# Attention on one Trainium2 core: scores in two pairs of PSUM banks, everything else in one shared bank, xn and y turned by DMA as fp16 halves

## The reference

```
x = x + attention(layernorm(x))     # 16 heads of 16 channels, causal, rotation by head index
x = x + moe(layernorm(x))           # shared SwiGLU + 8 experts, top 2 per token
attention: q, k, v = split(xn @ W_attn + b); softmax(q k^T / 4, causal) v; y @ W_proj + b_proj
```

## Time and profile before

| | |
|---|---|
| median of 3 runs | 1647.81 us (1647.56 to 1649.53) |
| profiled execution | 1641.4 us, its span 1639.7 us |
| mean granted TensorE clock | 0.976 |
| busy over the span | PE 1506.1 us (92%), DVE 1045.2 (64%), ACT 828.9 (51%), POOL 895.8 (55%) |
| attention stage | to about 814 us of the span; then shared and routed experts |

### The profile page before, as it was taken

How to read it: one execution, slowest core, us unless ns; L and a number is a source line. 1 busy time by engine, 2 the same in 40 slices (tenths; PEclk the granted TensorE clock), 3 DMA queues, 4 the chain that set the end, 5 groups by cost and what they waited for, 6 DMA issues and landing times.

```text
span 1639.7 us, 41525 instructions
## 1 busy us (share of the span) xinstructions
PE 1506.1 (92%) x14714; PEld 1099.9 (67%) x14716; DVE 1045.2 (64%) x1828; ACT 828.9 (51%) x1252; POOL 895.8 (55%) x1121
## 2 busy tenths in 40 slices
PE   3689999999999999987699999999999999999995
PEld 2345555555555555543577888889888888888884
DVE  7567888888888888877468887743333333333332
ACT  1266666666666666655223335534444444444442
POOL 2144555555555555544131777747666666666663
PEclk9699999999999999999699999999999999999998
DMA  2333333333333333344867954446666666666662
GB/s 84 97 92 91 116 99 115 106 104 117 94 109 112 110 105 111 97 118 103 169 164 213 221 114 99 92 111 104 105 99 101 101 99 105 98 103 97 103 101 37
DMA packets 283156, 181.03 MB, mean 110 GB/s; under 512 B 160625, under 2 KB 273649, under 8 KB 282962
## 3 DMA queue, kind: packets, MB, share of 16 engines
q1 hardware_dynamic: 244370, 130.25, 31.4%
q0 software_dynamic: 30016, 35.55, 14.9%
q10 hardware_dynamic: 8576, 12.58, 2.4%
HBM read 83.91 MB, written 60.17 MB: 88 GB/s over the span
## 4 chain that ended last, share of the span: by engine, by line
PE 62%; DVE 9%; DMA 9%; SPq 6%; issue 5%; POOL 4%; ACT 4%; ACTq 0%; POOLq 0%; DVEq 0%
PE bank L1582 19%; PE pair_s L1856 12%; PE bank L1717 6%; PE bank L1856 6%; PE pair_t L1856 6%; SPq L442 4%; PE pair_s L1644 4%; DMA qk_d<-qkl 3%; PE bank L1752 3%; PE pair_t L1691 3%; ACT prob L883 2%; DMA k_op<-qk_d 2%; POOL prob L685 1%; DVE early L1503 1%; POOL tok_d L767 1%
## 5 line engine op out<-in xcount | busy, mean ns | idle before, releaser
L883 ACT ACTIVATE prob<-pair_t 128x1024 f32<-128x1024 f32 x320 | 327.8, 1024 | 228.6 <-PE pair_t L1691 223.8
L685 POOL TENSOR_SCALAR_AFFINE_SELECT prob<-prob 128x256 f32<-128x256 f32 (+1 forms) x448 | 198.5, 457 | 330.5 <-ACT prob L883 322.6
L808 POOL DMA_INDIRECT out_x<-ysb,tok_rows x135 | 217.1, 1608 | 156.5 <-ACT ysb L1019 107.6
L992 ACT CAST early<-early 128x512 f16<-128x512 f32 (+1 forms) x206 | 124.3, 603 | 324.1 <-DVE early L1503 302.0
L1509 DVE TENSOR_TENSOR early<-early 128x512 f16<-128x512 f32 (+1 forms) x206 | 138.9, 674 | 137.9 <-ACT early L992 135.2
L1503 DVE SCALAR_TENSOR_TENSOR early<-pair_s,h_s,sg 128x512 f32<-128x512 f32 (+1 forms) x103 | 75.2, 730 | 226.5 <-PE pair_s L1856 215.8
L1582 PE MATMUL bank<-wbuf,early 128*128 x1620 | 188.7, 273 | 4.7 <-DVE early L1509 3.4
L1856 PE MATMUL pair_s<-xt,wbuf 128*128 128x256 f16 x1704 | 188.7, 267 | 2.3 <-ACT sg L984 1.4
L767 POOL DMA_INDIRECT tok_d<-tok_w,dest_i x128 | 135.4, 1058 | 99.2 <-DVE dest_i L1426 58.2
L1717 PE MATMUL bank<-prob,v_op 128*32 128x512 f32 (+3 forms) x2048 | 178.8, 444 | 5.1 <-POOL prob L685 5.0
L1158 DVE TENSOR_REDUCE mx<-pair_s 128x2 f32<-128x1024 f32 x128 | 156.8, 1225 | 41.0 <-PE pair_s L1664 40.2
(11 more groups left out here) (272 smaller groups left out, 2735.9 us busy)
## 6 DMA issues: line engine op xcount, KB each, us to landing
q_op<-qk_d SPq DMA_DIRECT2D x192, 64.0 KB, 2.6
k_op<-qk_d SPq DMA_DIRECT2D x192, 64.0 KB, 2.7
x_in<-in_L_attn_x SPq DMA_DIRECT2D x16, 512.0 KB, 3.9
qk_d<-qkh SPq DMA_DIRECT2D x32, 256.0 KB, 2.2
qk_d<-qkl SPq DMA_DIRECT2D x32, 256.0 KB, 2.6
xres<-in_L_attn_x SPq DMA_DIRECT2D x16, 512.0 KB, 4.6
x_d<-x SPq DMA_DIRECT2D x32, 256.0 KB, 2.2
xhl_d<-xhl SPq DMA_DIRECT2D x32, 256.0 KB, 2.5
```

What stands on the lines that cost most here:

```text
L685: last = nc.gpsimd.affine_select(out=v, in_=v, compare_op=ALU.is_ge, fill=0.0, base=0, pattern=[[0, v.shape[1]], [1, P]], channel_multipli ...
L808: pool.indirect_dma_start(out=out, out_offset=bass.IndirectOffsetOnAxis(ap=tok_rows[:, block, 0:1], axis=0), in_=ysb[:, here], in_offset=N ...
L883: nc.scalar.activation(prob[:, half, u].rearrange("p a n -> p (a n)"), pair_t[:].rearrange("p a n -> p (a n)"), ACT.Exp, scale=exp_by).the ...
```

## The change

It is one rewrite of the attention stage's plan with these parts.

1. PSUM: banks 5 and 6 become `pair_u`, and scores alternate between `pair_s` and `pair_u`; they wait for the maximum of the unit two before. Everything else (q/k and v projections, maxima, o, output projection: 16 uses a batch) goes through bank 7, `ps_a`, each use waiting for the one that last emptied it.
2. xn is split into fp16 halves by POOL (`xn_split`, a cast and a subtraction for each of four tiles) and turned by one transposing DMA of 512 KB on SP (`xn_columns`); `transpose_xn`, `xn_high` and `xn_low` go. W_attn is split into scaled fp16 halves instead of fp32r.
3. y is split the same way (`y_split`) and turned by two transposing DMAs of 256 KB (`y_columns`); `transpose_y` and ACT's copy go. The output projection becomes 12 fp16 matmuls for each half in place of eight fp32 ones; W_proj is scaled and split once, and the scales are taken off in `values`, `divide` and `residual`.
4. Exponentials and selections run two whole groups back (10 units in place of 8), the value products of a group at (2 groups later, unit 3) and (3 groups later, units 0, 0 and 1).
5. All slots are set anew. Stores of q and k are at (2,0) and (2,4), their loads start in the same slots; xn is turned at (0,0), y at (3,1) and at (0,0) of the batch after.
6. Variances stay in one array `mv_all`, which saves a copy; PE waits for the last x1 ahead of the shared expert.

```diff
+        pair_of = (pair_s, pair_u)
+        ps_t, ps_o, ps_a = bank[2:4], bank[4], bank[7]
...
-        LAG, MAXIMA, M_ROWS, M_SP, O_OUT = 8, 0, 1, 2, 3
-        MIX = (0, 2, 2, 3)
-        XN_T, XN_HIGH, XN_LOW = ((0, 1), (0, 2)), ((0, 1), (0, 2)), ((0, 1), (0, 3))
-        QK, QK_ROWS = ((0, 4), (1, 4), (2, 4), (3, 1)), ((1, 0), (2, 0), (3, 0), (3, 4))
-        QK_HIGH, QK_LOW = ((1, 1), (2, 1), (3, 1), (0, 0)), ((1, 2), (2, 2), (3, 3), (0, 1))
-        V_PROJ, V_PROJ_B, VALUES = ((1, 2), (2, 1)), ((1, 3), (2, 1)), ((1, 3), (2, 3))
-        QK_STORE, QK_LOAD = ((2, 3), (0, 2)), ((2, 3), (0, 3))
-        STATS, VARIANCE, RSTD, SHIFT = ((1, 0), (1, 2)), (1, 4), (1, 4), (2, 1)
...
-        O_T = ((1, 4), (2, 2), (3, 2), (0, 1))
-        Y_T, Y_OUT = ((2, 3), (0, 3)), ((3, 1), (0, 4))
-        PROJ, PROJ_B = ((3, 3), (1, 1)), ((3, 4), (1, 1))
...
+        MAXIMA, M_ROWS, M_SP = 1, 1, 2
+        MIX, O_OUT = ((2, 3), (3, 0), (3, 0), (3, 1)), (3, 1)
+        XN_SPLIT, XN_COLUMNS = ((1, 2), (2, 0), (3, 2), (3, 4)), (0, 0)
+        QK = QK_ROWS = ((0, 4), (1, 2), (1, 4), (2, 0))
+        QK_HIGH, QK_LOW = ((1, 0), (1, 3), (2, 0), (2, 2)), ((1, 1), (1, 4), (2, 1), (2, 3))
+        V_PROJ = VALUES = ((2, 4), (3, 3))
+        QK_STORE = QK_LOAD = ((2, 0), (2, 4))
+        STATS, VARIANCE, RSTD, SHIFT = ((0, 3), (0, 4)), (0, 4), (0, 4), (1, 0)
+        NORMALISE = ((1, 0), (1, 3), (2, 3), (3, 0))
+        O_T = DIVIDE = ((2, 2), (2, 3), (3, 0), (3, 2))
+        Y_SPLIT, Y_COLUMNS = ((2, 4), (3, 0), (3, 1), (3, 3)), ((3, 1), (0, 0))
+        PROJ = ((3, 4), (0, 2))
+        X_BIAS = ((1, 0), (1, 3), (2, 2), (3, 1))
+        X1, X1_STATS, X1_VARIANCE = ((3, 4), (0, 2)), ((0, 0), (1, 1)), ((0, 0), (1, 2))
+        RSTD_B, ROWS = ((0, 0), (1, 2)), ((0, 1), (1, 4))
+        XRES, ROWS_OUT = (0, 3), ((1, 1), (3, 2))
...
+            def xn_columns(n):
+                sp.wait_ge(S["xnl_done"], NT * (n + 1))
...
+                    sp.wait_ge(S["qk_in"], 4 * n)
+                    sp.wait_ge(S["v_in"], 2 * n)
...
+                sp.dma_start_transpose(xn_t[:], xn_hl[:].rearrange("p t n -> p (t n)")).then_inc(S["xn_cols"], 16)
...
+            def y_columns(bp, j):
+                sp.wait_ge(S["yl_done"], 4 * bp + 2 * j + 2)
...
+                    sp.wait_ge(S["pr_in"], 2 * bp + j)
...
+                sp.dma_start_transpose(y_t[:], y_hl[:, j].rearrange("p t n -> p (t n)")).then_inc(y_turned[j], 16)
...
+                high = xn_hl[:, t, 0:C]
+                nc.gpsimd.tensor_copy(high, xn[:, t]).then_inc(S["xnh_done"], 1)
...
+                nc.gpsimd.tensor_tensor(xn_hl[:, t, C:], xn[:, t], high, ALU.subtract).then_inc(S["xnl_done"], 1)
...
-                if some(UN * G + u):
-                    pe.wait_ge(S["max_done"], UN * G + u)
+                if some(UN * G + u - 1):
+                    pe.wait_ge(S["max_done"], UN * G + u - 1)
+                pair_k = pair_of[(UN * G + u) % 2]
...
+            def project_out(bp, j, nxt):
+                pe.wait_ge(y_turned[j], 16 * bp + 16)
...
+                    last = products(ps_a[:, 256 * t:256 * t + 256],
+                                    [((y_t[:, 4 * t + c, :], y_t[:, 4 * t + CC + c, :]), (wp_h[:, c, :], wp_l[:, c, :]))
+                                     for c in range(CC)])
```

More of the change, by code:

```diff
@@ L467, in _ @@
                         load_qk(0, 0, j, third, a)
+            xn_columns(1)
             sp.dma_start(gate_t[:], gate_w).then_inc(S["misc_in"], 16)
@@ L509, in body @@
                             sp.dma_start(xres[:], xv[b - 1]).then_inc(S["res_in"], 16)
+                        for j, bp in heads_here((g, s), Y_COLUMNS, b, prev, prev2):
+                            y_columns(bp, j)
+                        if nxt and prev and (g, s) == XN_COLUMNS:
+                            xn_columns(b + 1)
                         for j, bp in halves_here((g, s), ROWS_OUT, b, prev, prev2):
@@ L652, in _, with y_split @@
             input_rstd(1)
+            for t in range(NT):
+                xn_split(1, t)
+            pool.wait_ge(S["wp_in"], 1)
+            nc.gpsimd.partition_all_reduce(wp_top[:], wp_max[:], P, RMAX).then_inc(S["wp_topped"], 1)
+            def y_split(bp, q):
+                k, j = 4 * bp + q, q // 2
+                pool.wait_ge(S["y_done"], k + 1)
+                if q % 2 == 0 and some(bp):
+                    pool.wait_ge(y_turned[j], 16 * bp)
+                high = y_hl[:, j, q % 2, 0:C]
+                nc.gpsimd.tensor_copy(high, y[:, q % 2]).then_inc(S["yh_done"], 1)
+                pool.wait_ge(S["yh_done"], k + 1)
+                nc.gpsimd.tensor_tensor(y_hl[:, j, q % 2, C:], y[:, q % 2], high, ALU.subtract
+                                        ).then_inc(S["yl_done"], 1)
             def qk_high(n, i):
@@ L717, in body @@
                                 input_rstd(b + 2)
+                            for t in range(NT):
+                                if (g, s) == XN_SPLIT[t]:
+                                    xn_split(b + 2, t)
+                        for q, bp in heads_here((g, s), Y_SPLIT, b, prev, prev2):
+                            y_split(bp, q)
                         for j, bp in halves_here((g, s), RSTD_B, b, prev, prev2):
@@ L864, in prologue @@
                     normalise(0, 0, t)
-                for c in range(2):
-                    xn_high(0, c, XN_BANK[c])
                 act.wait_ge(S["scales_done"], 2)
@@ L1107, in prologue @@
                 link.link(dve, nc.vector.tensor_tensor(od, od, rope_t[:, 0], ALU.add))
-                for s in range(2):
+                for s in range(3):
                     last = nc.vector.tensor_reduce(qk_max[:, s:s + 1], wa[:, :, 256 * s:256 * s + 256],
@@ L1279, in body @@
                         if nxt:
-                            for c in range(2):
-                                if (g, s) == XN_LOW[c]:
-                                    xn_low(b + 1, c)
                             for j in range(2):
@@ L1562, in _, with columns @@
         def _(pe):
-            def transpose_xn(n, c, out=None):
-                pe.wait_ge(S["xn_done"], n + 1)
-                if out is None:
-                    out = ps_q
-                    if c:
-                        pe.wait_ge(S["xl_done"], 2 * n + c)
-                    else:
-                        pe.wait_ge(S["qkl_done" if n == 1 else "qkf_done"], 4 * n)
-                for t in range(NT):
-                    last = nc.tensor.transpose(out[:, P * t:P * (t + 1)], xn[:, t, P * c:P * (c + 1)], ident[:])
-                last.then_inc(S["xnT_in"], 1)
+            def columns(part, c):
+                return xn_t[:].rearrange("p (t a c) n -> p a c t n", a=2, c=CC)[:, part, c]
             def products(out, pairs):
@@ L1586, in project_qk @@
             def project_qk(n, i, out=None):
-                if out is not None or i == 0:
-                    pe.wait_ge(S["xl_done"], 2 * n + 2)
-                elif i < 3:
-                    pe.wait_ge(S["v_done"], 2 * n + i)
+                if out is not None:
+                    pe.wait_ge(S["xn_cols"], 16)
+                elif i == 0:
+                    pe.wait_ge(S["xn_cols"], 16 * n + 16)
+                    if n > 2:
+                        pe.wait_ge(S["x1_done"], 2 * (n - 2))
+                    elif n == 2:
+                        pe.wait_ge(S["m_done"], 4)
+                    else:
+                        pe.wait_ge(S["qkl_done"], 4)
+                elif i == 1:
+                    pe.wait_ge(S["m_done"], 4 * (n - 1) + 1)
                 else:
@@ L1611, in prologue @@
             def prologue():
-                for c in range(2):
-                    transpose_xn(0, c, XN_BANK[c])
                 pe.wait_ge(S["attn_w"], 2)
@@ L1618, in prologue @@
                     col = 256 * (i % 2) + P * (i // 2)
-                    last = nc.tensor.matmul(ps_m[:, i:i + 1], wa[0:1, 2, col:col + P], one[0:1, :],
+                    last = nc.tensor.matmul(bank[6][:, i:i + 1], wa[0:1, 2, col:col + P], one[0:1, :],
                                             start=True, stop=True)
```

347 lines of the change are left out of this document (184 added, 163 removed).

## The result

The changed kernel takes 1709.26 us (median of 4 runs, 1707.05 to 1713.93), the kernel before 1647.68 beside it: ratio 1.039, 95% interval 1.037 to 1.041. Forecast were 1637, in a range of 1588 to 1664.

What follows compares the result with a forecast made beforehand. TensorE bounded steady batches before; after the change SP's serial loop would, at 44.0 us. Loops -3.6, last batch -11, end +2 and start +2 sum to -10.6: 1631 us profiled, 1637 in the median, range 1588 to 1664.

Steps and rivals of the forecast that it cites:

- The sums of the engines: Busy time per steady batch: PE from 42.7 to 38.1 us, DVE from 37.9 to about 36.4, POOL under 33.
- The loop on SP: y_columns 1, output projection, POOL's qk_low, then SP's stores and loads: 44.0 us sets batches 2 to 13, -3.6 in all.
- "12.0" and "4.6": In the loop: PE from the projection to slot (1,4), 12.0 us; POOL's qk_low ending 4.6 us after that slot began.
- twice from the store to the first load: In the loop on SP: issuing each half's q/k store and waiting for its landing, 3.2 us each, 6.4 together.
- All else on SP: Other issues in the loop: 24 loads, maxima, y_columns 0, x1/xhl stores, load_x and one long issue; 17.3 us.
- Landing 3.7: y_columns 1 lands 3.7 us after issue, like the shared stage's 256 KB ones; bounds 2.6 and 5.4.
- rival B: Slower: y_columns 1, issued behind load_x's 512 KB, lands after 5.4 us; loop 46.5, total 1670; chance 0.25.
- The start: Batch 2's load comes behind xn_columns on SP and DVE asks for it earlier: +2 us, between 0 and +5.
- The last body: Batch 15: with two pairs of score banks PE need not wait for maxima: -11 us, between -6 and -13.
- The end: Two more units and a DMA round trip per half of y, logits' transposes alongside: +2 us, between -1 and +6.
- The shared bank: Bank 7's 16 uses per batch, each waiting for the one before: taken as 0, uncovered 4.8 us a batch.
- Rival A: SP's loop is slack and PE and DVE set about 39.0 us a batch: total 1576; chance 0.13.

Runs made afterwards that it cites:

- the last experiment: The fastest kernel with the scores in one pair of banks again, each unit's scores behind the maximum of the unit before: 1640.7 us, 0.999 of the kernel before.
- the fastest kernel: The changed kernel with half 1's q/k loads moved to the next batch, one partition reduction and the start reordered: 1610.21 us, 0.982 of the kernel before.

## Why the prediction was wrong, point by point

**The sums of the engines: right.** PE 38.1 a batch was forecast; it is 38.4 at clock 1.00 in the last experiment, 39.1 in the fastest kernel, and 40.7 at 0.94 in the changed one. DVE 36.4 forecast, 37.0 to 37.7 seen; POOL 32.3 forecast, 32.5 seen.

**The loop on SP: the right mechanism, mis-sized. This is the step that failed:** "Loop: 12.0 + 4.6 + 22.9 + 0.8 + 3.7 = 44.0 us", with its ends at 41.5 and 46.5. It is 48.5. The 4.5 us missing, twelve times, are 54 of the 57 us that lie between my -3.6 and the +53.5 of the 14 batches. Term by term:
- "12.0" and "4.6", PE and POOL to the store, took 18.5. (By its own terms the 4.6 is 4.35: 1.7 + 6.4 - 3.75.) I counted POOL from (1,2). In the chain above it is held at (0,4), by the small power that waits for DVE's statistics, which stand behind maxima and the residual; from 271.65 it works almost without a gap to 282.62. Where the projection runs at the lower clock, up to 1.3 us come on top (last section), 0.4 in the mean of the 11 loops.
- The 6.4 for "twice from the store to the first load" is 6.4: right.
- All else on SP is 18.9, not 17.3. The price of a load, six issues in 2.72 us, was of a good stretch; loads that took 0.6 to 2.1 us came one or two to a loop, and I added 0.8 once, so the 24 loads took 12.6 and not 11.7. I left out the waiting instructions and the short stops between issues, some 1 us a loop.
- "Landing 3.7" is 4.7. I had the cause as rival B and in the upper bound, and set the value by the same operation elsewhere, where no 512 KB go ahead of it. load_x behind y_columns 1 gives 3.5.

My bounds were narrow because every term was bounded by itself from rows of calm stretches; three of four erred to one side, and the measured loop lies 2 us above the upper end. Rival B had the side and one of the causes, the late landing behind load_x; its 1670 was still 39 short.

**The start: mis-sized, +20.1 for "+2, between 0 and +5".** I saw the added reduction in the change and priced POOL's splits, but not what lies between a reduction and a power on POOL. In the kernel before, the first change can lie beside DVE's work (its reduction follows DVE's last maximum by 0.13 us); the splits ahead of the reduction laid it open, and the second reduction added two more. One reduction gave back 9.3 of the 20.1; with the reordered start and the late loads the head of body 1 is at 90.3, 26.0 earlier than in the changed kernel.

**The last body: right in size,** -10.7 for -11; but with one pair again it is only 7.3 longer in the changed kernel, so the rest of the change gave some 3 of it, which I had put down to the second pair alone. **The end:** +4.1 for +2, inside -1 to +6.

**The shared bank at 0: small in the changed kernel, more once the loop is slack.** In the changed kernel the waits for y and qkf ahead of the maxima are 0.6 us a batch (6.3 in ten); in the fastest one the waits for v_op, y and qkf are 1.1 us a batch or more, well below the 4.8 that I gave as the uncovered price.

**What would show it.** As foretold, "idle time of 2 to 3 us ahead of the output projection" in each half is what the trace has, 3.0, and the DMA of y ends it; "PE busy near 39 of 44 us" is 40.7 of 48.8. "a granted clock under 1.00 in steady batches" was listed as a sign against; it is 0.94, and 0.98 in the fastest kernel, where the waits for y are gone.

**Rival A (39.0 with the loop slack): refuted in size.** With the loop slack a batch takes 42.7, since PE waits for ACT, DVE and the shared bank.

The Trainium skill's rule to turn blocks on TensorE where PSUM will do as the destination (page VectorE: DVE Perf Modes, section Rules for kernel authors) came out right for the changed kernel as written, which is slower than the kernel that turns on PE. It does not decide by itself: the fastest kernel here turns by DMA and beats both. No run here kept the transposes on PE beside the other parts of the change, so what the turning by DMA is worth on its own is not shown.

## What to carry to other kernels

When work leaves the full engine for a DMA, draw the loop that goes through the queue that issues it, and count every issue and every wait that stands in that queue between one turn and the next; then ask which of them need not stand there. Here the place of twelve loads that were needed more than ten slots later made the difference between 3.9% slower and 0.6% faster than the kernel before. And look at the order of two DMAs issued one behind the other: the small one that somebody waits for goes first.

## What the runs showed of the hardware that I had not expected

**POOL's change between the partition reduction and a power costs 5.7 to 7.6 us without any row for it:** 5.76 and 6.28 ahead of the reductions above; ahead of the powers 8.13, of which 7.6 lie behind the end of DVE's variance, and 7.41 behind the operand's arrival at 78.33. Ahead of that last power POOL had been idle since 59 us, and the 7.41 us came all the same, once the operand was there. In the kernel before POOL stood idle for 5.87 us ahead of its first reduction, and that one followed its operand by 0.13. The Trainium skill (page GPSIMD Engine Reference, section 2.1 Instruction dispatch) says that the first call of a freshly loaded kernel pays about 6 us, with no instruction of its own in the profile; the rows ahead of the reductions agree in size, those of the powers are longer, and what POOL does in that time no row here shows.

**A projection that follows a wait can run at half clock.** Three projections with the wait ahead of each, then stretches around the first two (columns as in the busy times by stretch; the last stretch holds two of the next matmuls as well):

```profile
263.57 2.74 PE L1636 MATMUL bank<-cs,y_t 128*128 128x256 f16 x12 [4.27 <-DMA y_t<-y_hl]
...
362.27 1.48 PE L1636 MATMUL bank<-cs,y_t 128*128 128x256 f16 x12 [1.50 <-DMA y_t<-y_hl]
...
459.49 1.48 PE L1636 MATMUL bank<-cs,y_t 128*128 128x256 f16 x12 [3.39 <-DMA y_t<-y_hl]
```
```profile
259.50:263.50 4.00, 0.00 (x0) 0.00 (x0) 2.22 (x5) 1.50 (x2) 1.29 (x4) 0.93 1.05 242
263.60:266.20 2.60, 2.60 (x12) 1.60 (x12) 0.00 (x0) 0.00 (x0) 0.00 (x0) 0.50 0.61 124
...
362.30:363.70 1.40, 1.40 (x14) 1.08 (x16) 0.00 (x0) 0.07 (x1) 0.47 (x2) 1.00 1.13 224
```

After 4.27 us without work the 12 matmuls took 2.74 us at a granted clock of 0.50 (1.2 GHz); after a wait of 1.50 they took 1.48 at 1.00 (2.4 GHz). The length of the wait alone does not decide it: after 3.39 us the 12 took 1.48 again. The loop goes through this projection, so a wait can be paid for twice: with up to 1.3 us more in each loop where this happens, which is five of the 11 loops, three of them in part.
